# Constant rows and zeros of the attention stacks written in other places, function tables brought in ahead, and tile numbers read in another split

## The reference, cut to what is computed

```
x = x + tanh(g_xattn[0]) * L0_xattn(layernorm(x), ctx)   # keys: 361 context rows + 100 own; 16 heads of 16
x = x + tanh(g_ffn[0])   * L0_ffn(layernorm(x))          # fake-quantised: silu(x Wg) * (x Wu), 704 wide, then Wd
x = x + tanh(g_xattn[1]) * L1_xattn(layernorm(x), ctx)   # keys: 361 context rows
x = x + tanh(g_ffn[1])   * L1_ffn(layernorm(x))          # top 2 of 8 experts, 256 -> 1024 -> 256, relu
```

## Time and profile before

| | |
|---|---|
| median of 3 runs | 696.75 us (691.8 to 701.3) |
| the profiled execution's own time | 700.24 us |
| its span | 698.5 us, mean granted clock 0.869 |
| TensorE busy | 514.7 us, 74% |
| TensorE weight loads | 355.1 us, 51% |
| VectorE busy | 437.9 us, 63% |
| ScalarE busy | 298.5 us, 43% |
| GpSimd busy | 146.5 us, 21% |

### The profile page before, as it was taken

How to read it: one execution, slowest core, us unless ns; L and a number is a source line. 1 busy time by engine, 2 the same in 40 slices (tenths; PEclk the granted TensorE clock), 3 DMA queues, 4 the chain that set the end, 5 groups by cost and what they waited for, 6 DMA issues and landing times. The chain is left out here.

```text
span 698.5 us, 15585 instructions
## 1 busy us (share of the span) xinstructions
PE 514.7 (74%) x5425; PEld 355.1 (51%) x5425; DVE 437.9 (63%) x918; ACT 298.5 (43%) x480; POOL 146.5 (21%) x184
## 2 busy tenths in 40 slices
PE   0381778879878988844537798989975158999994
PEld 0161345556556655733223365655554146788883
DVE  7724577666656676456962676777567873666652
ACT  1065324555555555502404265766753221333331
POOL 1200002111211121100032601112123032444432
PEclk9995968999999897877868788999986578999998
DMA  8030683444534550000044559699447111222310
GB/s 259 4 112 3 117 161 78 127 106 106 124 77 100 145 145 24 2 0 1 0 113 81 150 144 179 138 167 161 136 156 254 54 38 17 42 43 44 51 23 0
DMA packets 73247, 64.31 MB, mean 92 GB/s; under 512 B 33326, under 2 KB 65750, under 8 KB 73190
## 3 DMA queue, kind: packets, MB, share of 16 engines
q1 hardware_dynamic: 61816, 41.78, 26.4%
q0 software_dynamic: 8224, 21.06, 11.6%
q10 hardware_dynamic: 3152, 0.71, 0.5%
HBM read 48.59 MB, written 15.92 MB: 92 GB/s over the span
## 5 line engine op out<-in xcount | busy, mean ns | idle before, releaser
L458 PE MATMUL PS<-QS,KS 112*120 112x100 f16 (+2 forms) x896 | 93.0, 230 | 11.2 <-ACT PT L521 9.5
L458 PEld LDWEIGHTS PS<-QS,KS 112*120 112x120 f16 (+2 forms) x896 | 82.4, 144 | 36.6 <-ACT PT L521 15.1
L569 DVE CUSTOM_DVE_ANT_0 PS<-PS,maskv 100x461 f32<-100x461 f32 x128 | 80.4, 647 | 13.9 <-PE PS L427 12.6
L572 DVE TENSOR_REDUCE mx<-PS 100x1 f32<-100x361 f32 x128 | 63.6, 529 | 37.0 <-PE PS L430 35.8
L521 ACT ACTIVATE PT<-PS 120x400 f32<-120x400 f32 (+1 forms) x128 | 63.3, 503 | 37.1 <-PE PS L458 34.8
L521 ACT ACTIVATE PT<-PS,ctxb 120x400 f32<-120x400 f32 (+1 forms) x96 | 56.9, 594 | 49.8 <-PE PS L458 48.5
L427 PE MATMUL PS<-KS,QS 65*100 65x461 f16 x128 | 51.6, 408 | 15.6 <-DVE mx L569 15.1
L2003 PE MATMUL PS<-WE,hidden_high 128*128 x160 | 55.4, 391 | 5.7 <-issue 5.7
L1990 PE MATMUL PS<-aT,WE 128*128 128x128 f16 x960 | 59.3, 221 | 0.0
L779 POOL TENSOR_SCALAR_AFFINE_SELECT PT<-PT 100x400 f32<-100x400 f32 x32 | 17.7, 554 | 190.8 <-ACT PT L521 190.8
L1990 PEld LDWEIGHTS PS<-aT,WE 128*128 x960 | 56.6, 99 | 0.5
(11 more groups left out here) (302 smaller groups left out, 1062.3 us busy)
## 6 DMA issues: line engine op xcount, KB each, us to landing
share<-in_L_ffn_w_dram POOLq DMA_DIRECT2D x13, 1024.0 KB, 8.5
k_scratch<-share SPq DMA_DIRECT2D x32, 180.5 KB, 2.5
KS<-k_scratch SPq DMA_DIRECT2D x32, 180.5 KB, 3.7
KS<-k_scratch SPq DMA_DIRECT2D x64, 90.2 KB, 5.8
QS<-q_scratch SPq DMA_DIRECT2D x64, 50.0 KB, 2.6
v_scratch<-xn SPq DMA_DIRECT2D x8, 385.7 KB
values_staged<-v_scratch SPq DMA_DIRECT2D x8, 385.7 KB
WE<-in_L_ffn_w_dram POOLq DMA_DIRECT2D x2, 1024.0 KB, 8.8
```

Of the source, the lines that this page charges most:

```text
L458: last = nc.tensor.matmul(bank[0:kn, i * T:(i + 1) * T], KS[p][:, h, k0:k0 + kn], QS[p][:, h, :], start=True, stop=True)
L569: nc.vector.tensor_tensor_reduce(rows, rows, maskv[:, :], 1.0, -BIG, ALU.add, ALU.max, mx[p][:, h:h + 1]).then_inc(s_smf, 1)
L572: nc.vector.tensor_reduce(mx[p][:, h:h + 1], sm_bank[h % 2][0:T, 0:TC], X, ALU.max).then_inc(s_smf, 1)
```

## The change

In the opening: VectorE clears both query stacks and only the first half (heads 0 to 7, HM = 8) of the first key stack ahead of the statistics; the other three halves stand behind the low halves of x, behind the small value clearings, and behind the scaling of the clip factors. ScalarE writes the constant rows of both key stacks first of all. GpSimd's clearings wait until the rows are normalised. In the second and third block ScalarE runs a silu and an exp on one column of a tile that nobody reads any more (`gts`), before it waits for anything (the silu stands behind the attention's transposes). In the last block TensorE reads 2 numbers with their checks first and 18 without checks later, and from the third tile on `hidden` waits for all 16 weight steps instead of for those of its own expert.

```
                 pool_rstd(pool, 0)
+                pool.wait_ge(s_xn, NTILE)
                 for p in range(2):
                     nc.gpsimd.memset(Vc[p][:, :, :, :], 0.0)
...
                     act.dma_start(dst, src, allow_slow_non_contiguous=k <= 4).then_inc(s_bias, 16)
+                act.wait_ge(s_dl, 1)
+                for p in range(2):
+                    nc.scalar.activation(KS[p][IROW:KX, :, :], delta[:, :].unsqueeze(2).to_broadcast([H, H, S0]), ACT.Copy
+                                         ).then_inc(s_kr, 1)
                 act.wait_ge(s_wr[0], 16)
                 nc.scalar.activation(wah[:, :, :], r_attn, ACT.Copy, scale=WS).then_inc(s_wh8, 1)
...
                     wide_hi(act, 4 + mb, skh[:, mb, :], bcol[:, 1, mb:mb + 1])
-                act.wait_ge(s_dl, 1)
-                for p in range(2):
-                    nc.scalar.activation(KS[p][IROW:KX, :, :], delta[:, :].unsqueeze(2).to_broadcast([H, H, S0]), ACT.Copy
-                                         ).then_inc(s_kr, 1)
...
             def _(dve):
                 for p in range(2):
                     nc.vector.memset(QS[p][KROWS:IROW, :, :], 0.0)
-                    nc.vector.memset(KS[p][KROWS:IROW, :, :], 0.0)
+                nc.vector.memset(KS[0][KROWS:IROW, 0:HM, :], 0.0)
                 dve.wait_ge(s_x, 32)
...
                     wide_lo(dve, kc, xTh[:, kc, :], xTl[:, kc, :])
+                nc.vector.memset(KS[0][KROWS:IROW, HM:H, :], 0.0)
...
                 nc.vector.memset(Vs[:, :, :, DH:VW], WS)
+                nc.vector.memset(KS[1][KROWS:IROW, 0:HM, :], 0.0)
...
                 nc.vector.tensor_scalar(clipt[:, :], clipt[:, :], 1.0, 0.5 / QMAX, ALU.add, ALU.mult)
+                nc.vector.memset(KS[1][KROWS:IROW, HM:H, :], 0.0)
...
                     act_attT(act, kc, f"a{kc}")
+                nc.scalar.activation(gts[:, 0:1], gts[:, 0:1], ACT.Silu)
                 act.wait_ge(s_sc, 1)
...
             def _(act):
+                nc.scalar.activation(gts[:, 1:2], gts[:, 1:2], ACT.Exp)
                 for kc in range(KC):
                     wide_hi(act, U[f"q_x{kc}"], xTh[:, kc, :])
...
-                def hidden(a, ready):
+                def hidden(a, ready, behind_all=False):
...
-                    pe.wait_ge(s_wlo, ready)
+                    pe.wait_ge(s_wlo, NWS if behind_all else ready)
...
-                steps_in(0, 4)
+                _, v = nc.values_load_multi_w_load_instructions(
+                    ew[0:1, 0:2], engines=[mybir.EngineType.PE], min_val=NWS - 2 * (E - 1), max_val=NWS)
+                er = list(v)
...
                 hidden(1, er[1])
-                steps_in(4, NS)
+                _, v = nc.values_load_multi_w_load_instructions(
+                    ew[0:1, 2:NS], engines=[mybir.EngineType.PE], min_val=NWS - 2 * (E - 1), max_val=NWS,
+                    skip_runtime_bounds_check_because="NWS less twice a count of 0 to E - 1 comparisons")
+                er.extend(v)
                 outcome(0, er[0])
...
-                        hidden(a + 1, er[a + 1])
+                        hidden(a + 1, er[a + 1], True)
```

33 lines of the change are left out of this document (19 added, 14 removed).

## The result

| | before | after |
|---|---|---|
| median of 4 runs | 698.69 us (691.8 to 701.3) | 681.02 us (677.38 to 682.58) |
| span of the profiled execution | 698.5 us | 675.7 us |
| mean granted clock in it | 0.869 | 0.874 |

What follows compares the result with a forecast made beforehand. No engine is full, so each edit is worth what its own stretch waits for. Opening -14.35, silu table -1.3, exp table -0.3, reads -1.8 sum to -17.75 us: 696.75 to 679.0 us, range 673 to 687.

Steps and rivals of the forecast that it cites:

- The opening, -14.35 us: Clearings and constant rows moved, up to the first attention: first context half at 52.95 instead of 67.30 us.
- dear clearings: Rival, chance 0.22: each half clearing costs 4.60 us, TensorE stays slow in its projections, reads worth 0; about -12 us.
- the rival's 2 us for a slow first phase: In the opening's projections: TensorE, idle longer beforehand, stays slow, costing 2 us; part of a rival given 0.22.
- VectorE's 14.8 us: At the first product: what VectorE alone would give; forecast only -7.9 us there, as ScalarE is late next.
- Silu and exponential, -1.3 and -0.3: Table loads moved off the first feed-forward silu and the second attention's first exponential: -1.3 and -0.3 us.
- the rival of a drain: At both table switches: each costs its 1.28 us and as much again unseen; sum -21.4 us, chance 0.02.
- The reads, -1.8: Behind the second expert tile: 18 unchecked numbers make TensorE's stall 3.8 us instead of 5.67, gain 1.8 us.
- The 0.35 us of VectorE's row: VectorE's stall between two tiles, reading one number; taken to match 0.21 for the read plus 0.14 for checks.
- the rival that I gave 0.12: At the expert tiles: reads nearly free and clock kept, -5.3 - 2.9 us there, sum -24, 673 us; chance 0.12.
- The clock, 0: Behind the second expert tile: the clock's fall may be missed, worth up to 2.9 us; taken as 0.
- the 5 us at which I had said I would be wrong: Sign of failure: the attention loops change their length by over 5 us.
- Part 5: Expert tiles in the last block: the reads' edit, -1.8 us; the wait on a constant in 18 tiles frees nothing.

Runs made afterwards that it cites:

- the repeat: The changed kernel run once more, unchanged, as a control: 681.2 us median, ratio 0.9781 to the kernel before.
- the kernel with the clearings only: The kernel before with VectorE's moved clearings and GpSimd's wait, ScalarE's constant rows still behind the projections: 688.79 us, ratio 0.9857.

## Why the prediction was right, and where it was not

**The opening, -14.35 us: right in the mean, and right by all its steps but one.** Statistics 6.5 forecast and 6.59 read; rows 11.4 and 11.44; constant rows from 6.95 and from 7.20; first product 24.75 and 25.03; third clearing's end 42.0 and 41.07; first context half 52.95, and 52.07 to 53.30 in the profiles of kernels with this opening (52.18, 53.04, 53.09, 53.30, 52.30, 52.07). Their mean, 52.66, makes it -14.6. The price of a half clearing, 3.85 against the 4.60 of the other reading, is 3.94 as measured: dear clearings fall. One thing was not foreseen and cost nothing: the biases' scaling took 3.39 us beside GpSimd's clearings, hidden only because ScalarE led. Another was not foreseen and moves single profiles. From the first product to VectorE's last own-key half I kept the old length, 12.94 us; it took 11.69 in the first profile of the change, 12.99 in the repeat, and 11.65 to 12.99 in the six. That, and not the clearings, spreads the first context half over 1.2 us and brought the third clearing's end to 41.07. It goes with TensorE's pace: its 512-column products follow each other at 0.43 us at first and at 0.21 later, from 37.9 on before (5.2 us after the first product) and from 27.5 on in the change (2.5 us after it), although the granted clock reads 1.00 in both stretches. So the rival's 2 us for a slow first phase after the longer pause are not there: no profile was over 0.05 us longer than before. That VectorE's 14.8 us would not all arrive because ScalarE is late next was the step that mattered, and the kernel with the clearings only shows its other half.

**Silu and exponential, -1.3 and -0.3: right**, 1.30 and 0.34 read. No second microsecond went with either table load. The exponential shows it at its own start: it came 2.86 us after the maximum rows began in the kernel before and 1.57 us after them in the change, 1.29 us sooner, of which 0.34 was left at the fourth. So the rival of a drain falls: by the Trainium skill (ScalarE: Activation LUTs, What ACT_TABLE_LOAD costs) about 1.4 us more would have gone with each, and no run here shows it.

**The reads, -1.8: the size nearly right (-1.43), the working wrong.** The step that failed is the sentence that no row times the read or a check alone. The rows were in the trace of before, 1.11 us for the load of 16 and 0.146 for a check's register operations. I put 3.4 us on the load and 2.3 on the checks; it was 1.1 and 4.6. The 0.35 us of VectorE's row that seemed to confirm the split prices no read: its bracket names TensorE's product as what ended it, and VectorE's own load of one number takes 0.30 us and the register operations of its check another 0.19. With those rows my own method would have given 18 x 1.11 / 16 = 1.25 us of pause, -4.4 us and more with the clock: the rival that I gave 0.12. And that would have been wrong too, since a load that starts off 16 bytes costs 3.2 us more. The two errors cancelled by luck. For a read of 16 from number 4 that rival comes true: the pause 1.07, the clock kept, 21.88 - 14.56 = 7.3 us.

**The clock, 0: right as far as the runs can tell.** From the first turn to the fourth 2.12 us went, 1.43 of it the pause. The other 0.7 us go with the clock: it was low from about 577.3 to 584.2 before and from 553.5 to 560.3 in the change, 5.9 us of it under the products behind the pause before and 4.1 in the change. That isn't shown to be the shorter pause's doing. The kernel with the clearings only has the reads of before; its pause was 5.77 us, the clock fell 3.4 us ahead of its end instead of 1.0, and the rest of the stretch took 15.06 us, less than before (16.21) and than the change (15.52). In the loops the clock moved the first profile by 5.9 us and the repeat by 5.3. By the letter that is over the 5 us at which I had said I would be wrong; but the first loop alone moved by 4.6 us between two executions with the code of before, so I had set this sign within what unchanged code does by itself. That the clock averages out in the median is a reading; the runs of one kernel lie 5 to 14 us apart, which leaves some microseconds either way.

**The sum.** -14.35 - 1.3 - 0.3 - 1.8 = -17.75, against -14.6 - 1.3 - 0.34 - 1.43 = -17.7 from local readings (-18.4 with the 0.7 at the tiles) and -17.7 and -15.8 us from the two sets of medians. That the first of these meets the forecast to 0.1 us is partly luck. The forecast lay 3.8 us beyond the 2% that a measurement can tell, not the 3.7 of the prediction.

**What stays open.** What sets where in the loops, in the opening and behind the second tile TensorE is slow; that the first loop's length follows the clock is shown, why two executions of the same instructions differ is not. Whether groups of four are the hardware's or made when the load is built can't be seen in these traces. Part 5's wait on a constant was not tried alone.

## What to carry to other kernels

Before a cost is split by an estimate, ask the trace for the source line itself, with its sequencer instructions: register loads and checks are there even where the timeline shows only "issue". When an edit moves work out of one chain, look at which engine is late next both ahead of the old place and behind it; the value is the difference of two chains, not the length of what moved. In a kernel whose clock moves by phase, price edits by local readings between fixed events, and leave the span to the median.

## What the hardware showed that I had not expected

TensorE's register load depends on where it starts: 16 numbers took 1.11 us from number 4 and 3.81 us from number 2, 8 bytes into a group of 16; 18 took 1.61 from number 0 and 4.28 from number 2. The Trainium skill (DMA: Bandwidth & Descriptors, Latency and other measured facts) gives a load a floor of about 600 ns and says that the compiler unrolls it by four; here four numbers took 0.51 us and one, on VectorE, 0.30, under that floor. The Trainium skill's other figure (Runtime: NRT & Kernel Launch, Instruction fetch mechanics), about 200 ns a register even in bulk, which I had weighed, is given there for the registers that a launch loads from HBM; on these loads from SBUF it fits numbers outside of a four (0.22) and is four times too high inside one (0.05).

A bounds check costs 0.29 us of TensorE's sequencer, so 16 of them are longer than the read that they guard.
